# A two-layer expert kernel: the down product runs one step later, and VectorE adds its bias from a table

## What is computed

```python
top_vals, top_idx = jax.lax.top_k(x @ router_weight, 2)
scores = jax.nn.softmax(top_vals, axis=-1)
gu = jnp.einsum('th,ehf->tef', x, gate_up_proj) + gate_up_proj_bias      # 8 experts, 256 -> 512
gate, up = jnp.minimum(gu[..., ::2], 7.0), jnp.clip(gu[..., 1::2], -7.0, 7.0)
act = (up + 1.0) * (gate * jax.nn.sigmoid(gate * 1.702))                 # 256 wide
down = jnp.einsum('tei,eih->teh', act, down_proj) + down_proj_bias       # 256 -> 256
out = jnp.einsum('te,teh->th', w, down)                                  # w: the two scores of a token
```

## Time and profile before

| | |
|---|---|
| runs | 927.1, 920.6, 916.6 us, median 920.62 |
| the profiled execution | 910.28 us, of it 908.5 us between the first and the last instruction (span) |
| mean granted TensorE clock | 0.923 of full speed |
| first expert layer, first x transposes to last y in SBUF | 123.6 to 367.0 us of the span |
| second expert layer, the same | 619.0 to about 867.5 us |

### The profile page before, as it was taken

One profiled execution on the slowest core, in us unless ns is written; L12 is line 12 of the kernel. 1 busy time (PEld: TensorE's weight loads), 2 busy tenths in 40 slices (PEclk: granted clock), 3 DMA queues, 4 the chain that ended last, 5 costly groups with the idle time before them and its releaser, 6 DMA issues.

```text
span 908.5 us, 13906 instructions
## 1 busy us (share of the span) xinstructions
PE 679.6 (75%) x4026; PEld 572.0 (63%) x4027; DVE 493.4 (54%) x1096; ACT 302.4 (33%) x644; POOL 418.2 (46%) x423
## 2 busy tenths in 40 slices
PE   2473668989999999277777799374989998999900
PEld 2473647777777778155556599373777777777800
DVE  6567723444444444489997288762344444444448
ACT  2253213333333333144445144222333333333300
POOL 5264054667566653156668300006556656564310
PEclk9999999999999999699999699657999999999965
DMA  7452021222222230333331243102222222222159
GB/s 272 149 185 83 1 70 59 77 76 85 75 80 80 75 75 36 116 93 104 104 105 44 85 143 113 47 1 81 68 68 70 85 70 80 75 80 69 42 180 374
DMA packets 40953, 85.80 MB, mean 94 GB/s; under 512 B 10045, under 2 KB 17234, under 8 KB 40405
## 3 DMA queue, kind: packets, MB, share of 16 engines
q1 hardware_dynamic: 19688, 41.29, 13.5%
q0 software_dynamic: 13856, 35.69, 12.1%
q10 hardware_dynamic: 7376, 8.42, 2.6%
HBM read 51.76 MB, written 35.69 MB: 96 GB/s over the span
## 4 chain that ended last, share of the span: by engine, by line
PE 56%; DVE 18%; issue 12%; DMA 6%; ACT 2%; POOL 2%; another core or an unknown queue 2%; DVEq 1%; SPq 0%; POOLq 0%; ACTq 0%
PE ps L735 12%; PE ps L736 11%; PE ps L737 11%; PE ps L727 9%; PE ps L731 6%; DVE xs L1197 5%; DVE work L1022 3%; DMA work<-y_dram 2%; PE ps L753 2%; PE ps L782 2%; PE ps L781 2%; DVE bst L1006 2%; DMA xn_dram<-work 2%; DVE work L1224 1%
## 5 line engine op out<-in xcount | busy, mean ns | idle before, releaser
L456 POOL DMA_INDIRECT work<-xn_dram,gidx x144 | 145.2, 1008 | 170.8 <-DVEq L1152 125.7
L464 POOL DMA_INDIRECT y_dram<-work,sidx x144 | 144.6, 1004 | 171.6 <-ACT work L609 136.5
L727 PE MATMUL ps<-cst,work 128*128 128x128 f32 x832 | 140.2, 296 | 82.1 <-DVE work L1022 64.6
L727 PEld LDWEIGHTS ps<-cst,work 128*128 128x128 f32 x832 | 105.8, 152 | 102.4 <-DVE work L1022 58.1
L731 PE MATMUL ps<-biases,ones 128*128 (+2 forms) x352 | 119.3, 339 | 60.6 <-issue 27.2
L735 PE MATMUL ps<-up_hi,xT_hi 128*128 x288 | 142.7, 496 | 0.0
L1157 DVE TENSOR_TENSOR xT_lo<-ps,xT_hi 128x512 fp32r<-128x512 f32 x72 | 49.8, 691 | 155.5 <-ACT xT_hi L590 126.8
L736 PE MATMUL ps<-up_lo,xT_hi 128*128 x288 | 115.0, 399 | 0.0
L737 PE MATMUL ps<-up_hi,xT_lo 128*128 x288 | 114.4, 397 | 0.0
L1162 DVE TENSOR_TENSOR aT_lo<-ps,aT_hi 128x512 fp32r<-128x512 f32 x72 | 49.7, 691 | 92.3 <-ACT aT_hi L595 60.3
L731 PEld LDWEIGHTS ps<-biases,ones 128*128 128x128 bf16 x352 | 34.7, 99 | 102.4 <-issue 77.3
(11 more groups left out here) (135 smaller groups left out, 1297.4 us busy)
## 6 DMA issues: line engine op xcount, KB each, us to landing
work<-y_dram SPq DMA_DIRECT2D x32, 512.0 KB, 4.1
xs<-L_attn_x SPq DMA_DIRECT2D x4, 1024.0 KB, 6.2
work<-L_ffn_gate_up_proj SPq DMA_DIRECT2D x8, 512.0 KB, 3.7
xn_dram<-work SPq DMA_DIRECT2D x16, 256.0 KB, 3.4
q_dram<-work ACTq DMA_DIRECT2D x16, 256.0 KB, 3.0
work<-q_dram SPq DMA_DIRECT2D x16, 256.0 KB, 2.8
xn_dram<-work ACTq DMA_DIRECT2D x16, 256.0 KB, 2.0
out<-xs SPq DMA_DIRECT2D x16, 256.0 KB, 5.4
```

Source lines behind the costliest of these rows:

```text
L456: pool.indirect_dma_start(xg[:, k, u, :], None, xn_dram[n], bass.IndirectOffsetOnAxis(ap=gidx[:, 2 * s + u:2 * s + u + 1], axis=0)).then_i ...
L464: pool.indirect_dma_start(y_dram[n], bass.IndirectOffsetOnAxis(ap=sidx[:, 2 * s + u:2 * s + u + 1], axis=0), ysb[:, k, u, :], None, bounds ...
L727: ins = nc.tensor.transpose(ps[:, bank, k:k + P], src[:, u, c * P:(c + 1) * P], ident)
```

## The change

- `down` runs one step later: in step s TensorE does down(s-2) instead of down(s-1), after up(s, 1). So the numbers of the experts are kept in four pairs of registers, and `aT` gets a second buffer, for which the tensors `xn1` (used by the attention alone) serve. The transposes of act now wait for `a_lo` of the step before (bank 6), `down` for y of the step before (bank 7), and `a_hi` for the down product two steps back.
- The bias product of `down` is gone. A table `dn_b` of all eight down biases (8 x 256 fp32), the same on all 128 partitions, is loaded by SyncE with one 1 MB DMA from DRAM in each layer, issued when the routing is done. VectorE waits for it after its first `activate`.
- `y_out` moves from ScalarE to VectorE: it reads the two expert numbers into registers, waits for `y_ps`, and adds bank 7 and the table, one instruction per tile, into `ysb`. `ysb` has two buffers instead of four.
- ScalarE's order in a step is x_hi(s+1), gelu of u = 0, a_hi(s-1), gelu of u = 1, and its loop has two steps. VectorE's is x_lo(s+1), clip 0, a_lo(s-1), clip 1, product, y_out(s-2).
- The down biases are taken out of the rows that are split at the start: `biases` is 4864 instead of 6912 wide, and one of its small DMAs is gone on ScalarE's and on SyncE's queue.
- After the last step TensorE does down(34), transposes of act of 35, down(35).

The core of the diff:

```diff
-        ysb = area(4608, RING, 2, H)
+        ysb = area(4608, 2, 2, H)
+        dn_b = area(5632, E, H)
+        aTb = [[t[:, :, :, :] for t in aT],
+               [t[:, :, :, :].rearrange("p b u h -> p (b u h)")[:, 0:2 * KC * P].rearrange(
+                   "p (u c t) -> p u c t", u=2, c=KC) for t in xn1]]
...
+            def load_down_bias(n):
+
+                sp.wait_ge(L[n].routed, 1)
+                sp.dma_start(dn_b.rearrange("p e h -> p (e h)"),
+                             bdn.rearrange("(a e) h -> a (e h)", a=1).to_broadcast([P, E * H])).then_inc(dn_b_loaded, 16)
...
-                    k = s % RING
+                    k = s % 2
                     pool.wait_ge(l.y_sb, s + 1)
...
-                def y_out(s, k, rounds):
-                    act.wait_ge(l.y_ps, s + 1)
-                    wait(act, l.scattered[k], 32 * rounds)
-                    nc.scalar.activation(ysb[:, k], ps[:, 7, :].rearrange("p (u h) -> p u h", u=2),
-                                         ACT.Copy).then_inc(l.y_sb, 1)
...
+                def step(s, b):
                     if not (isinstance(s, int) and s + 1 >= NP):
                         x_hi(s + 1, 1 - b)
-                    a_hi(s - 1)
-                    glus(s, b)
-                    y_out(s - 1, d, it)
+                    half_glu(s, b, 0)
+                    a_hi(s - 1, 1 - b)
+                    half_glu(s, b, 1)
...
                     pe.wait_ge(l.act, s + 1)
+                    wait(pe, l.a_lo, s)
                     transpose4(6, act_v[:, b]).then_inc(l.a_T, 1)
 
-                def down(s, e):
+                def down(s, b, e):
                     pe.wait_ge(l.a_lo, s + 1)
+                    wait(pe, l.y_sb, s)
                     for u in range(2):
                         o = ps[:, 7, u * H:(u + 1) * H]
-                        bias(o, e[u] * H + B_DN, H)
...
                     a_transpose(s - 1, 1 - b)
                     up(s, b, 1, e[1])
-                    down(s - 1, e_last)
-                    return e
+                    if not (isinstance(s, int) and s < 2):
+                        down(s - 2, b, named((d + 3) % RING))
...
+                def activate(s, b, between=None):
+                    clip(s, b, 0)
+                    if between is not None:
+                        between()
+                    st.done(clip(s, b, 1))
                     v.scalar_tensor_tensor(out=act_v[:, b], in0=glu[:, b], scalar=GLU_LIMIT, in1=upv[:, :, :],
                                            op0=ALU.min, op1=ALU.mult).then_inc(l.act, 1)
+
+                def y_out(s, b, rounds):
+
+                    dve.load(names, expert[0:1, bass.ds(s * 2, 2)])
+                    e = [dve.snap(r, min_val=0, max_val=E - 1) for r in names]
+                    dve.wait_ge(l.y_ps, s + 1)
+                    wait(dve, l.scattered[b], 32 * rounds)
+                    for u in range(2):
+                        ins = v.tensor_tensor(ysb[:, b, u, :], ps[:, 7, u * H:(u + 1) * H],
+                                              dn_b[:, bass.ds(e[u], 1), :].rearrange("p a h -> p (a h)"), ALU.add)
+                    ins.then_inc(l.y_sb, 1)
...
+                        activate(s, b, lambda: a_lo(s - 1, 1 - b))
+                        if not (isinstance(s, int) and s < 2):
+                            y_out(s - 2, b, it - (d == 0))
+                st.loop(NP // 2 - 1, 2, body, peel=2)
```

More of the change, by code:

```diff
@@ L118, in stages, with loop @@
             step(g, g % 4, g // 4)
-    def loop(self, count, per, body):
+    def loop(self, count, per, body, peel=1):
         base = self.n
-        body(0)
-        with self.eng.Fori(1, count) as it:
+        for it in range(peel):
+            body(it)
+        with self.eng.Fori(peel, count) as it:
             self.n, self.done_in_body = base + it * per, 0
@@ L591, in x_hi, with a_hi @@
                                          ACT.Copy).then_inc(l.x_hi, 1)
-                def a_hi(s):
+                def a_hi(s, b):
                     act.wait_ge(l.a_T, s + 1)
-                    nc.scalar.activation(aT[0][:, :, :, :], ps[:, 6, :].rearrange("p (u c t) -> p u c t", u=2, c=KC),
+                    wait(act, l.y_ps, s - 1)
+                    nc.scalar.activation(aTb[b][0], ps[:, 6, :].rearrange("p (u c t) -> p u c t", u=2, c=KC),
                                          ACT.Copy).then_inc(l.a_hi, 1)
-                def glus(s, b):
-                    wait(act, l.act, s - 1)
-                    for u in range(2):
-                        act.wait_ge(l.gu, s * 2 + u + 1)
-                        nc.scalar.activation(glu[:, b, u, :],
-                                             ps[:, 2 + 2 * b + u, :].rearrange("p (f c) -> p f c", c=2)[:, :, 0],
-                                             ACT.Gelu_apprx_sigmoid).then_inc(l.glu, 1)
@@ L624, in body @@
                 def body(it):
-                    for d in range(RING):
-                        step(it * RING + 1 + d, d, it)
-                repeat(act, (NP - 1) // RING, body)
-                for s in range((NP - 1) // RING * RING + 1, NP):
-                    step(s, (s - 1) % RING, (s - 1) // RING)
-                a_hi(NP - 1)
-                y_out(NP - 1, (NP - 1) % RING, (NP - 1) // RING)
+                    for d in range(2):
+                        step(it * 2 + 1 + d, 1 - d)
@@ L633, in _ @@
+                repeat(act, NP // 2 - 1, body)
+                step(NP - 1, 1)
+                a_hi(NP - 1, 1)
             gates(L[0])
@@ L783, in route @@
                     ins.then_inc(l.hot_used, 1)
[L785 removed]
+            names = [[pe.alloc_register(f"expert_{k}{u}") for u in range(2)] for k in range(RING)]
             def experts(l):
@@ L811, in up @@
                         pe.wait_ge(l.x_lo, s + 1)
-                    else:
-                        wait(pe, l.y_sb, s - 1)
                     o = ps[:, 2 + 2 * b + u, :]
@@ L1152, in route, with experts @@
                 v.engine_nop().then_inc(l.routed, 1)
-            def experts(l):
+            names = [dve.alloc_register(f"expert_{u}") for u in range(2)]
+            def experts(l, n):
                 def x_lo(s, b):
@@ new lines, in clip @@
+                def clip(s, b, u):
+                    if u == 0:
+                        wait(dve, l.act, s)
+                    dve.wait_ge(l.glu, s * 2 + u + 1)
+                    return v.tensor_scalar(upv[:, u, :],
+                                           ps[:, 2 + 2 * b + u, :].rearrange("p (f c) -> p f c", c=2)[:, :, 1],
+                                           1.0 - LIMIT, 1.0 + LIMIT, ALU.max, ALU.min)
+                def activate(s, b, between=None):
[3 more added lines that the diff above has]
+                    st.done(clip(s, b, 1))
```

98 lines of the change are left out of this document (49 added, 49 removed).

## The result

The changed kernel took 934.45 us, the median of four runs (930.83 to 937.93), where the kernel before took 923.86 us beside it (916.6 to 930.34). The ratio is 1.019, with an interval from 1.013 to 1.025. So it is slower by 1.9%, where 6% faster was forecast, and it lies outside the range.

A forecast was written before the change was run, and what follows sets the result against it. TensorE, with stalls it gets from others, was taken to bound the expert layers. 30.0 (shorter steps) + 34.4 (stalls) - 4 (table) - 3.5 (layer end) = 57 us, median 920.6 to 864; 8-in-10 range 842 to 892.

The forecast's parts named there:

- The clean step: TensorE's expert step without stalls: 5.92 to 5.52 us, 0.35 from the bias product and 0.05 from the gap before down.
- Table and tail: Losses per layer: table load beside the first gathers, 4 us in all; longer end of layer, 3.5 in all.
- the rival by which it holds the gathers up for the full 6.2: Layer start: the table load delays the first gathers by 6.2 us, 8 us less gain, 872 us; chance 0.08.
- the smaller bias rows: Kernel start: fewer bias rows to split, put at nothing because TensorE does not wait for them.
- So 17 of the 51.4 us stay and 34.4 go: TensorE's stalls in the two expert layers: of 51.4 us, 17 remain and 34.4 are gained.
- the ten late gelus: ScalarE's gelus starting late, 2.1 us idle on average; charged 1.2 each, 12 us, bounds 0 and 21.4.
- by 3 us and more: With down one step later, delays of x_hi, a_hi and y are covered by this slack; only act stays tight.
- all stalls vanish: Rival: late starts come with TensorE's waiting or fit the slack; 17 us more gain, 847 us; chance 0.15.
- close, the next bound ... nothing: GpSimd's gathers and scatters: 5.1 us a step, 92% of 5.52; later scatters priced at nothing.
- which it can hide behind: VectorE's register load in y_out hides behind the product of act; at worst it adds 0.54 + 0.1 us.
- The change doesn't help: late starts grow as the step shrinks: Rival: all 51.4 us of stalls stay with 15 more, gain 7.5 us, 913 us; chance 0.05.
- VectorE as the chain at 7.1 us a step: Rival: y_out waiting for late y_ps holds up VectorE's queue; 36 us slower, 957 us; chance 0.05.

The follow-up runs named there:

- e6: Kernel before with GpSimd's gathers replaced by plain SyncE loads of wrong rows, scatters kept: 851.76 us, ratio 0.933.
- e16: Kernel before with down one step later and GpSimd's gathers held until the step's second up product: 852.18 us, ratio 0.992.
- e5: Changed kernel with GpSimd's gathers replaced by plain SyncE loads of wrong rows, scatters kept: 828.71 us, ratio 0.908.
- e17: Changed kernel itself, run again on a chip where the kernel before takes 860.76 us: 832.90 us, ratio 0.968.
- e2: Kernel before without down's bias product, with table, y_out on VectorE and two y buffers, down not shifted: 922.38 us, ratio 1.008.
- D and E: Two groups of follow-up runs, each on one chip, where the kernel before took 858.44 and 860.76 us.
- e15: Changed kernel with a 512-word GpSimd write between each step's gathers and scatters: 866.95 us, ratio 1.011.
- e10: Changed kernel with the scatters as plain SyncE stores to wrong places, gathers kept: 837.04 us.
- e3: Changed kernel with GpSimd's gathers of s+4 held until the second up product of s is done: 876.60 us, ratio 0.957.
- e11: Changed kernel without y_out's register load, fixed table rows and so a wrong bias: 914.78 us, ratio 1.001.
- e18: Changed kernel with the load of expert numbers moved to the head of VectorE's step: 830.74 us, ratio 0.965.
- e7: Changed kernel with plain SyncE loads for the gathers and a 512-word GpSimd write in each gather's place: 831.32 us.
- A, B, C: Three groups of follow-up runs, each on one chip, where the kernel before took 914.86, 915.84 and 913.88 us.
- e8: Changed kernel with indirect gathers of 64 values a row instead of 256, from wrong rows: 933.17 us.

## Why the prediction was wrong

- **The clean step held.** 5.52 was forecast, 5.49 is there. The gain of the 34-step stretches is 402.7 - 370.3 = 32.4 us, where the text had 30.0. Its parts were sized the wrong way round: the bias product gives 0.28 a step, not 0.35 (389.0 - 370.3 over 68), and the shift 0.15, not 0.05 (5.92 to 5.77). Of that 0.05 is the gap before `down` (0.29 us after the last up product in e6, 0.24 in e16), and `down` itself takes 1.68 instead of 1.76; the rest I can't place.
- **Table and tail came near in the sum, not in the parts.** Forecast was a loss of 7.5 us. With no stalls in either, the span goes from 849.5 (e6) to 826.2 (e5), 23.3 us, so 9.1 of the 32.4 are given back; in the profiled executions of before and after the rest grew by 2.0 only. The first transposes come 4.4 (after) to 4.9 us (e17) after the first gather is issued, before it was 4.25; so the table's load costs 0.2 to 0.6 us and not the 2 that I took, and the rival by which it holds the gathers up for the full 6.2 did not come. After the last up product the last y is in SBUF after 9.6 us (e17), where 8.6 was forecast and 6.9 was before. And the smaller bias rows, put at nothing, bring the first gather some 2 us forward, from 119.35 to 117.22 (e2, which has the table but the rows of before, starts it at 119.91). That the sum fits is in part luck.
- **The step that failed is "So 17 of the 51.4 us stay and 34.4 go".** 102.5 us of stalls are there, 85 more than the 17. All of the miss of the profiled execution is in it: 931.0 - 853.3 = 77.7 = 85.5 - 2.4 (the stretches' gain) - 5.5 (the rest went up by 2.0, not by 7.5). The place was right: the rest of the idle stands before the transposes of act, released by VectorE's product. The size rested on the ten late gelus and their 2.1 us of the earlier trace rows, taken as given. But they were no constant of the machine. Their number went to 25, their mean to 2.6, and x_hi and y, which I called covered "by 3 us and more", started late 17 and 13 times (9 and 4 before), after idles of up to 4.1 us. The text said itself "What delays these starts no row says", and then gave them a price for the new order. The bounds given for it, 0 and 21.4 us, held only if the late starts stayed as many as they were, and nothing in the rows says that.
- **The same stalls told more than I read in them.** 51.3 us is nearly all of the difference between the chips for the kernel before: 914 to 924 against 858 to 861. That they lie only where GpSimd issues gathers was visible in the earlier trace rows: the four steps at the end of a layer have none. I used it for the rival "all stalls vanish" and did not follow it to GpSimd.
- **GpSimd "close, the next bound ... nothing"** was mis-sized. It was put at 5.1 us of 5.52. In e17 its round is 5.49 us: the idle between its instructions is 0.30, 0.30, 0.58 and 0.31 instead of 0.26 each. It is full. The price of nothing was right on the chips of D and E, but GpSimd has no reserve: with one write of 0.57 us more in its round the whole kernel follows (e15: 35 us). On the other chips the two kernels that take work off its queue, e5 and e10, lose nearly all stalls, and the one that spaces it, e3, half.
- **The register load**, "which it can hide behind" the product, takes 0.61 us and not 0.54, and costs some 17 us on a chip with late signals (e11). Without them it is hidden as I said: TensorE is busy through both stretches of e17, and an earlier place of the load changes 2 us, which can't be told from none (e18). How it costs 17 us beside late signals is not shown.
- **The rivals.** "The change doesn't help: late starts grow as the step shrinks" named what happened, at 0.05 and with 15 us more where 51 came (102.5 - 51.3). The one on the slower side was VectorE as the chain at 7.1 us a step; VectorE has 3.5 us of work in a step of 7, and it waits with everyone else.

**What stays open.** Why TensorE's signals are late on some chips and not on others is not shown. Each chip was used in one group only, so a lasting property of the chip is not told from a state that it was in at the time. The profiler recorded each execution here (each has a span and a granted clock), and those of the first sort lack records; whether the recording takes part in the delays was not tested. That the late signals need the indirect DMAs of GpSimd is shown (e5 and e6 with two executions each, e7 and e10 with one); that their number rises with the length of GpSimd's runs is only seen side by side. That y starts later, that GpSimd's DMAs bunch behind it, and that the bunch then delays the next signals would explain why the stalls double, and why the pause helps; this circle, and with it the reason why this change lengthens the stalls, is argued, not shown. Nor is it settled whether the load costs 17 us by its place or wherever it stands: the two runs meant for it fell on chips without late signals.

## What to carry to other kernels

Idle time that a profile puts to nobody is a cause that you have not found: find which engine's signals are late and in which phases before you give it a price in a new order, and until then leave the range open on both sides. A gain from a shorter step is real only if nothing else grows with the pace; compare the stretch with as many clean steps as it holds, in before and after. And if a change loses against its own clean steps, run it on a second chip before you judge it: this change makes the kernel 1.9% slower on one and 3.2% faster on another. A trace that lacks the landings of its indirect DMAs was the mark of the first sort.

## What the runs showed of the hardware

- **Two sorts of chip.** 43 runs of the kernel before in four groups (this result's, A, B, C) took 905 to 930 us, 23 in two groups (D, E) 856 to 863, with no overlap. The changed kernel's two profiled spans differ by 98.2 us (929.2 and 831.0), its two stretches by 102.5. The granted clock is alike, 0.918 in e17 and 0.914 on the first chip.
- **TensorE's signals can be up to 5.6 us late.** Normally a signal is out 0.01 us after the modelled end of the product. The Trainium skill (TensorE: Matmul & The Clock Gate, The cost: per-tile semaphore tail) gives, for packed tiles, a tail of 25 ns plus 4.7 for each tile and 26.3 for each increment. For one tile and one increment that makes 56 ns, an estimate by that page; e17 stays below it (no signal of its products over 0.02 us behind the modelled end), the changed kernel on the first chip far above (5.6 us between the end of the product at 181.41 and its gelu at 187.04). Only TensorE's signals do that (all records of VectorE, ScalarE and GpSimd in that trace lie within 0.02 us of the end of an instruction), only in phases in which GpSimd issues indirect DMAs, and several are let through together.
- **TensorE's clock fell to 1.2 GHz behind its own idle time**: ten times, behind idles of 2.3 to 3.8 us, in the two stretches of the changed kernel on the first chip, and not at all in those of e3 and e17.
- **An indirect DMA costs GpSimd 1.0 us and 0.3 more before the next can start**, 1.3 to 1.4 us in all, whether it moves 256 values a row or 64 (e8: 0.98 us on average for the gathers). Two gathers and two scatters are 5.5 us.
- **A register load of two values takes 0.61 us on VectorE** (0.52 to 0.78), and 0.54 on TensorE.
